# A reordered step in a one-core layer pipeline: three shared PSUM banks, a copied row buffer, a folded normalisation

## What is computed

```python
x = _ln(src) * (1.0 + scale) + shift          # scale, shift from the timestep
q, k, v = x @ Wq + bq, x @ Wk + bk, x @ Wv + bv
scores = q @ k.T / 4 + attention_bias         # per entry and head, 256 x 256
scores = where(src_mask, -inf, scores)
ctx = softmax(scores) @ v
x = x + (ctx @ Wo + bo)
h = _ln(x) * g2 + beta2
return x + _gelu2(h @ W1 + b1) @ W2 + b2      # _gelu2(z) = z * sigmoid(1.702 z), 1024 wide
```

## Time and profile before

| | us |
|---|---|
| median of 3 runs (lowest, highest) | 1541.29 (1540.1, 1541.68) |
| the profiled execution: its time | 1540.95 |
| its span, first to last instruction | 1539.2 |

### The profile page before, as it was taken

How to read it: one execution, slowest core, us unless ns; L and a number is a source line. 1 busy time by engine, 2 the same in 40 slices (tenths; PEclk the granted TensorE clock), 3 DMA queues, 4 the chain that set the end, 5 groups by cost and what they waited for, 6 DMA issues and landing times.

```text
span 1539.2 us, 37068 instructions
## 1 busy us (share of the span) xinstructions
PE 1305.6 (85%) x9217; PEld 1126.9 (73%) x9217; DVE 1207.3 (78%) x3280; ACT 979.0 (64%) x2358; POOL 722.3 (47%) x629
## 2 busy tenths in 40 slices
PE   2666599999999999982799998898988889999985
PEld 2555488888888888872678777777776777878875
DVE  3887899999999999976577777676775776777763
ACT  2222488888888888850666666565664666666761
POOL 1677488888888888863122223221332132222111
PEclk9999999999999999995899999898999999999997
DMA  3675333333343343326765566454663565556510
GB/s 113 226 238 198 134 130 127 126 132 124 125 133 125 124 133 126 129 81 221 227 188 184 160 196 189 149 168 141 186 201 124 172 185 165 173 166 188 172 56 14
DMA packets 195251, 236.53 MB, mean 154 GB/s; under 512 B 20448, under 2 KB 176288, under 8 KB 195168
## 3 DMA queue, kind: packets, MB, share of 16 engines
q1 hardware_dynamic: 182512, 198.51, 41.4%
q10 hardware_dynamic: 6480, 20.32, 4.1%
q0 software_dynamic: 6176, 16.79, 3.2%
HBM read 195.84 MB, written 39.71 MB: 153 GB/s over the span
## 4 chain that ended last, share of the span: by engine, by line
PE 29%; ACT 8%; DVE 8%; issue 7%; POOL 1%; SPq 1%; DVEq 0%; ACTq 0%; DMA 0%; POOLq 0%
PE ps_p L1258 5%; PE ps_g L1369 5%; PE ps_g L1326 4%; ACT bias L1158 4%; PE ps_ctx L1274 3%; PE ps_s L1244 3%; DVE bias L1459 2%; PE ps_g L1359 2%; PE ps_g L1315 2%; PE ps_s L1246 2%; DVE up_f L1542 2%; PE ps_g L1296 1%; ACT act_hi L1203 1%; PE ps_g L1316 1%; POOL act_lo L1117 1%
## 5 line engine op out<-in xcount | busy, mean ns | idle before, releaser
L351 POOL TENSOR_TENSOR w_lo<-w,w_hi 128x512 fp32r<-128x512 f32 x284 | 422.6, 1518 | 100.4 <-ACT w_hi L412 100.4
L1158 ACT ACTIVATE bias<-bias,neg_max 128x256 f32<-128x256 f32 x512 | 255.6, 501 | 203.9 <-DVE neg_max L1459 202.3
L714 DVE TENSOR_TENSOR w_lo<-w,w_hi 128x512 fp32r<-128x512 f32 x284 | 302.1, 1102 | 1.0 <-ACT w_hi L406 1.0
L1459 DVE CUSTOM_DVE_ANT_0 bias<-ps_s,bias 128x256 f32<-128x256 f32 x512 | 193.2, 415 | 32.2 <-issue 20.9
L412 ACT ACTIVATE w_hi<-w 128x512 fp32r x284 | 179.3, 633 | 54.0 <-PE ps_y L507 35.9
L1099 POOL TENSOR_TENSOR rstd<-mv,minus_half 128x2 f32<-128x2 f32 x32 | 23.1, 723 | 391.2 <-DVE mv L1517 305.4
L1244 PE MATMUL ps_s<-mask_f,minus_ident 128*128 128x256 f32 x512 | 156.6, 327 | 48.2 <-DVE neg_max L1459 31.0
L406 ACT ACTIVATE w_hi<-w 128x512 fp32r x284 | 173.3, 633 | 21.5 <-DVE tile_tab L683 11.0
L1258 PE MATMUL ps_p<-const,bias 128*128 128x128 f32 x1024 | 163.1, 283 | 23.8 <-ACT bias L1158 22.1
L507 PE MATMUL ps_y<-w_hi,hidT_hi 128*128 128x256 f32 x568 | 168.9, 297 | 14.9 <-DVE hidT_lo L700 14.2
L1117 POOL TENSOR_TENSOR act_lo<-up_f,act_hi 128x512 fp32r<-128x512 f32 x64 | 84.3, 1318 | 188.3 <-ACT act_hi L1203 188.3
(11 more groups left out here) (244 smaller groups left out, 3380.0 us busy)
## 6 DMA issues: line engine op xcount, KB each, us to landing
bias<-bias_dram SPq DMA_DIRECT2D x128, 512.0 KB, 3.7
b_row<-b_dram SPq DMA_DIRECT2D x71, 512.0 KB, 3.5
w<-w_dram ACTq DMA_DIRECT2D x32, 512.0 KB
xin<-dispatch SPq DMA_DIRECT2D x71, 128.0 KB, 2.2
b_row<-b_dram SPq DMA_DIRECT2D x71, 128.0 KB, 3.1
expert_out<-xin SPq DMA_DIRECT2D x71, 128.0 KB, 1.7
q_stack<-q_hi_rows SPq DMA_DIRECT2D x64, 128.0 KB, 3.3
k_stack<-k_hi_rows SPq DMA_DIRECT2D x64, 128.0 KB, 3.4
```

The source lines that it names most:

```text
L351: pool.tensor_tensor(w2_part["lo"][:, k, :], w2_piece(e, k), w2_part["hi"][:, k, :].bitcast(F32), ALU.subtract).then_inc(sem("w2_split"), 1)
L714: dve.tensor_tensor(w1_part["lo"][:, k, :], w1_piece(e, k), w1_part["hi"][:, k, :].bitcast(F32), ALU.subtract).then_inc(sem("w1_split"), 1)
L1158: act.activation(head_rows(h, j), head_rows(h, j), ACT.Exp, scale=-1.0, bias=neg_max[par][:, h, j:j + 1], accum_out=total[par][:, h, j:j + ...
L1459: dve.tensor_tensor_reduce(head_rows(h, j), ps_s[h % 2][:, j * T:(j + 1) * T], head_rows(h, j), -1.0, LARGEST, ALU.add, ALU.min, neg_max[p ...
```

## The change

- General banks: `ps_g` (2) and one of the two context banks give way to `ps_out`, `ps_k`, `ps_q`; the feed-forward's pairs use `ps_q` and `ps_k` (`ps_up`). The context of both halves goes to one bank.
- Order of a step on PE: q at 0, k at 2, `output` at 3, `values` at 4, `turn_h` at 6, `feed_up` at 7 to 10 as before, `feed_down` at 11 to 14, `turn_x` of entry n+2 at 15. On the other engines what follows moves with it: `modulate` of n+2 at 15; `upper` and `lower` of q at 1 and of k at 3; `scale_ctx` at 2; `combine_first` at 11, `combine_second` 12, `input_moments` 13, `normalise` 14; `finish` of entry n-1 at slot 15 of the same step rather than slot 0 of the next. `BY_VECTOR` has five heads.
- The modulated rows `xmT` have one buffer instead of two; a DMA on SP copies them to `xmT_kept`, from where `output` takes them.
- POOL's step: `take_mask`, `gather`, `rsqrt` of `rstd2`, `prepare_sum` (from DVE), the four `lower_gelu`, `rsqrt` of `rstd`. SP's step: `keep_rows` and `send_parts` come ahead of `load_bias(n, 6)`, and `bring_stacks` ahead of `load_bias(n, 7)`; what stands ahead of `load_mask` is as before.
- g2, beta2 and b1 are folded into W1 once: each row of W1 is scaled by g2, and the sum of b1 and beta2 - g2 times W1, over D, is added to each row, while `take_hT` adds 1 to the normalised rows, whose sum over D is nought. So `take_up` and `take_hT`'s scale and shift go, `tanh` and `gelu` read PSUM, and `take_hT` is one instruction that writes the upper part. The fold takes one more 512 KB load, four PE matmuls, and seven DVE instructions, in step -1, slot 6; `prepare_rest` moves there from slot 14.

```diff
...
-BY_VECTOR = (2, 3, 13, 15)
+BY_VECTOR = (0, 7, 8, 9, 10)
...
-    xmT = [sb(f"xmT{i}", [P, C, T]) for i in range(2)]
+    xmT = sb("xmT", [P, C, T])
+    xmT_kept = [sb(f"xmT_kept{i}", [P, C, T]) for i in range(2)]
...
-    ps_ctx = [bank(f"ps_ctx{i}") for i in range(2)]
-    ps_g = [bank(f"ps_g{i}") for i in range(2)]
+    ps_ctx = bank("ps_ctx")
+    ps_out, ps_k, ps_q = [bank(n) for n in ("ps_out", "ps_k", "ps_q")]
+    ps_up = [ps_q, ps_k]
+    b1_row = probT[:, 0:2, :, :].rearrange("p h j t -> p (h j t)")
+    less_gain = probT[:, 2, :, :].rearrange("p j t -> p (j t)")[:, 0:C * P].rearrange("p (c m) -> p c m", c=C)
...
+        def keep_rows(n, par):
+            sp.wait_ge(sem("xmT_ready"), C * (n + 1))
+            wait_free(sp, sem("wo_done"), n - 1, alone=True)
+            sp.dma_start(xmT_kept[par][:], xmT[:]).then_inc(sem("xm_kept"), 16)
...
                 if starting:
                     load_bias(n + 1, 0)
+                keep_rows(n + 1, 1 - par)
+                send_parts(n + 1)
             if exists(n):
                 load_bias(n, RING + 2)
             if exists(n + 1):
-                send_parts(n + 1)
+                bring_stacks(n + 1, 1 - par)
             if exists(n):
                 load_bias(n, RING + 3)
-            if exists(n + 1):
-                bring_stacks(n + 1, 1 - par)
             if exists(n + 1):
                 for c in range(1 if starting else 0, RING):
                     load_bias(n + 1, c)
...
+        def prepare_sum(n):
+            pool.wait_ge(sem("x3_ready"), n + 1)
+            wait_free(pool, sem("out_sent"), 16 * n)
+            pool.tensor_tensor(x3b[:], x3[:], spread(b2[:], [P, J, D], 1), ALU.add).then_inc(sem("x3b_ready"), 1)
         def step(n, par):
+            if exists(n + 1):
+                take_mask(n + 1, 1 - par)
+            if exists(n + 2):
+                gather(n + 2)
             if exists(n - 1):
                 rsqrt(rstd2, mv2, "var2_ready", "rstd2_ready", n - 1)
-            if exists(n + 2):
-                gather(n + 2)
-            if exists(n + 1):
-                take_mask(n + 1, 1 - par)
-            if exists(n - 1):
+                prepare_sum(n - 1)
                 for pair in range(4):
                     lower_gelu(n - 1, pair)
             if exists(n + 2):
...
-        def modulate(n, par):
+        def modulate(n):
             act.wait_ge(sem("xnT2_done"), n + 1)
             act.wait_ge(sem("entry_cols"), 4 * (n + 1))
-            wait_free(act, sem("wo_done"), n - 1)
+            wait_free(act, sem("v_done"), n)
+            wait_free(act, sem("xm_kept"), 16 * n)
             for c in range(C):
-                act.activation(xmT[par][:, c, :], ps_g[1][:, c * T:(c + 1) * T], ACT.Identity, bias=mod_now[:, 1, c:c + 1],
+                act.activation(xmT[:, c, :], ps_k[:, c * T:(c + 1) * T], ACT.Identity, bias=mod_now[:, 1, c:c + 1],
                                scale=mod_now[:, 0, c:c + 1]).then_inc(sem("xmT_ready"), 1)
...
         def take_hT(n):
             act.wait_ge(sem("h_turned"), n + 1)
-            wait_free(act, sem("hT_split"), n)
-            for c in range(C):
-                act.activation(hT[:, c, :], ps_g[1][:, c * T:(c + 1) * T], ACT.Identity, bias=vec[:, LN2_B + c:LN2_B + c + 1],
-                               scale=vec[:, LN2_G + c:LN2_G + c + 1]).then_inc(sem("hT2_ready"), 1)
+            wait_free(act, sem("ff1_done"), 4 * n)
+            act.activation(hT_part["hi"][:], halves(ps_k[:, :]), ACT.Identity, bias=1.0).then_inc(sem("hT_upper"), 1)
         def tanh(n, pair):
-            act.wait_ge(sem("up_ready"), F * n + 2 * pair + 2)
+            act.wait_ge(sem("ff1_done"), 4 * n + pair + 1)
             wait_free(act, sem("gelu_ready"), 4 * n + pair - 1)
             at = 2 * pair % 4
-            act.activation(tanh_f[:, at:at + 2, :], up_f[:, at:at + 2, :], ACT.Tanh, scale=0.851).then_inc(sem("tanh2_ready"), 1)
+            act.activation(tanh_f[:, at:at + 2, :], halves(ps_up[pair % 2][:, :]), ACT.Tanh, scale=0.851).then_inc(sem("tanh2_ready"), 1)
...
+                    modulate(n + 2)
                 if exists(n + 1):
+                    if isinstance(n, int) and n == -1 and h == 1:
+                        act.wait_ge(sem("setup_done"), 1)
+                    if h == 1:
+                        upper(n + 1, "q", ps_q, q_b)
                     if h == 3:
-                        modulate(n + 1, 1 - par)
-                    if h == 4:
-                        upper(n + 1, "q", 1, q_b)
-                    if h == 5:
-                        upper(n + 1, "k", 0, vec[:, K_B:K_B + C])
+                        upper(n + 1, "k", ps_k, vec[:, K_B:K_B + C])
                 if exists(n - 1):
...
         def turn_inv(n):
             pe.wait_ge(sem("inv_ready"), n + 1)
-            wait_free(pe, sem("up_ready"), F * n)
+            wait_free(pe, sem("result_ready"), n)
...
+            pe.wait_ge(sem("xm_kept"), 16 * (n + 1))
             for j in range(J):
...
         def feed_up(n, pair):
             if pair == 0:
                 pe.wait_ge(sem("hT_split"), n + 1)
-            elif pair == 1:
                 if exists(n + 2):
                     pe.wait_ge(sem("v_ready"), J * (n + 3))
-            else:
-                pe.wait_ge(sem("up_ready"), F * n + 2 * (pair - 1))
+            elif pair >= 2:
+                pe.wait_ge(sem("gelu_ready"), 4 * n + pair - 1)
             for i in range(2):
...
+        def fold_norm():
+            pe.wait_ge(sem("less_gain_ready"), 1)
+            for i in range(2):
+                for c in range(C):
+                    last = pe.matmul(ps_p[i][:, :], less_gain[:, c, :], w1_raw[c][:, i * 512:(i + 1) * 512],
+                                     start=(c == 0), stop=(c == C - 1))
+            last.then_inc(sem("norm_folded"), 1)
...
                         output(n - 1, 1 - par)
                 if exists(n + 1):
+                    if isinstance(n, int) and n == -1 and h == 0:
+                        pe.wait_ge(sem("setup_done"), 1)
+                    if isinstance(n, int) and n == -1 and h == 6:
+                        fold_norm()
+                    if h == 0:
+                        query_or_key(n + 1, "q", wq, ps_q)
                     if h == 2:
-                        turn_x(n + 1)
+                        query_or_key(n + 1, "k", wk, ps_k)
                     if h == 4:
-                        query_or_key(n + 1, 1 - par, "q", wq, 1)
-                    if h == 5:
-                        query_or_key(n + 1, 1 - par, "k", wk, 0)
-                if exists(n - 1) and h == 6:
-                    turn_h(n - 1)
-                if exists(n + 1) and h == 6:
-                    values(n + 1, 1 - par)
+                        values(n + 1)
                 if exists(n - 1):
+                    if h == 6:
+                        turn_h(n - 1)
                     if 7 <= h < 11:
                         feed_up(n - 1, h - 7)
-                    if h >= 12:
-                        feed_down(n - 1, h - 12)
+                    if 11 <= h < 15:
+                        feed_down(n - 1, h - 11)
+                if exists(n + 2) and h == 15:
+                    turn_x(n + 2)
                 if h % GROUP == 1:
                     before, head = neighbour(n, h, -GROUP - 1)
                     if exists(before):
                         weigh(before, head // GROUP, par if head < H - GROUP else 1 - par)
...
         def split_hT(n):
-            dve.wait_ge(sem("hT2_ready"), C * (n + 1))
-            wait_free(dve, sem("ff1_done"), 4 * n)
-            dve.tensor_copy(hT_part["hi"][:], hT).then_inc(sem("hT_upper"), 1)
             dve.wait_ge(sem("hT_upper"), n + 1)
-            dve.tensor_tensor(hT_part["lo"][:], hT, hT_part["hi"][:].bitcast(F32), ALU.subtract).then_inc(sem("hT_split"), 1)
...
-        def take_up(n, pair):
-            dve.wait_ge(sem("ff1_done"), 4 * n + pair + 1)
+            dve.scalar_tensor_tensor(hT_part["lo"][:], halves(ps_k[:, :]), 1.0, hT_part["hi"][:].bitcast(F32),
+                                     ALU.add, ALU.subtract).then_inc(sem("hT_split"), 1)
+        def gelu(n, pair):
+            dve.wait_ge(sem("tanh2_ready"), 4 * n + pair + 1)
             wait_free(dve, sem("act_split"), 4 * n + pair - 1)
-            for i in range(2):
-                f = 2 * pair + i
-                dve.tensor_scalar(up_f[:, f % 4, :], ps_g[1 - pair % 2][:, i * T:(i + 1) * T], vec[:, FF_B1 + f:FF_B1 + f + 1], None,
-                                  ALU.add).then_inc(sem("up_ready"), 1)
...
-            dve.wait_ge(sem("tanh2_ready"), 4 * n + pair + 1)
             at = 2 * pair % 4
-            dve.scalar_tensor_tensor(up_f[:, at:at + 2, :], tanh_f[:, at:at + 2, :], 1.0, up_f[:, at:at + 2, :],
+            dve.scalar_tensor_tensor(up_f[:, at:at + 2, :], tanh_f[:, at:at + 2, :], 1.0, halves(ps_up[pair % 2][:, :]),
...
```

(64 more changed lines are left out.)

78 lines of the change are left out of this document (36 added, 42 removed).

## The result

The changed kernel takes 1616.15 us (median of 4 runs, 1612.97 to 1622.43) where the kernel before takes 1541.49 beside it: 1.0485 times as long, 95% interval 1.0449 to 1.0522. Its profiled execution took 1622.43 us, 6 above its median, with a span of 1620.7 and a mean granted clock of 0.932 (before 0.967). The forecast was 1625.

The account below looks back on a forecast made before the run. PE sets the pace, but POOL's late root would hold it up: 13 x 54.0 + 4 x 4.5 = 720.0 instead of 639.8, +80.2, and +3.4 elsewhere, on 1540.95 give 1624.6, or 1625 us (1595 to 1660).

Parts of the forecast that it names:

- POOL's list decides: In POOL's step, `rstd2` stands behind late mask and gather, so `normalise2` ends at 24.1 while PE idles from 17.6.
- my upper end: Mask's landing after SP issues it: 3.0 us taken, upper value 3.7, as it starts behind bias chunk and result.
- Pure PE time and small waits, 40.5 + 1.05: Full step on PE: 40.5 us of work, plus waits of 0.25 for `xmT` and 0.8 for `feed_down`.
- rival 1: POOL is not late: `rstd2` answered at 14.6 to 15.5, step 43.2 us, total 1484, faster; chance 0.12.
- The delay, +9.4: Before `feed_up` in each full step: start at 28.4 instead of 18.95, +9.4 us, bounds 8.1 and 10.1.
- The clock, 3.0: PE's clock falls after 6.5 us idle ahead of `turn_h`, costing 3.0 us a step, bounds 0 and 5.
- rival 3: POOL late and PE at half clock through `feed_up`: 58 us a step, 1690 in all; chance 0.12.
- The step, 54.0: A full transformer step goes from 46.75 to 54.0 us, bounds 48.8 and 58.
- `feed_down`'s wait, 0.8 (0 to 1.4): PE's new wait at `feed_down`'s second quarter for the last `lower_gelu`: 0.8 us, less than 1.3 if `gelu` gets faster.
- The loop ends, 4 x 4.5 left: At four passes of the loop's end, 4.5 us each would remain of 7.8, between 1.3 and 7.8.
- The start, +11: Ahead of the first `minimum`, the fold's added work on DVE and PE delays the start by 11 us (9 to 14).
- Steps 14 and 15 and the tail, -7.6: Step 14, without `gather`, gains 1.6 us, step 15 gains 3, the last feed-forward 3.

Follow-up runs that it names:

- e12_after_again: The changed kernel, unchanged, run again beside the kernel before in a session on another chip: 1616.32 us, ratio 1.0342 to before.
- the fastest version: Changed kernel with POOL's root first, plus ACT taking `hT` and the last `upper_gelu` earlier and DVE the last lower part: 1480.51 us.

## Why the prediction was right, and where it was not

- **POOL's list decides: right, and shown from both sides.** Undoing it gains 119 us, doing it alone in the kernel before costs 54, or about 80 beside a before without ACT's unnamed wait. Counted from T0 = 1110.47, the chain ran: mask issued at 11.8 (forecast 11.1), taken by POOL 3.7 later (3.0, with 3.7 as the upper bound), `mask_f` 1.5, copies and gather 6.5, root 0.75, `turn_h` at 26.0 (24.1). The rest of that difference is one term I had at 0.73: the two normalisations, the second of which is held up beside POOL's `prepare_sum`, took 1.67. That this is the cause, the sum moved late shows: 0.73 again.
- **"DMA: Bandwidth & Descriptors", Two DMAs through the same engine are not ordered.** The Trainium skill's rule put the landing nearer to my upper end, and the trace agrees: counted as in the earlier trace rows, the mask landed in 3.5 us in the median (shortest 3.4), where a bias chunk took 3.6 in the same trace and 3.7 in before.
- **Pure PE time and small waits, 40.5 + 1.05: too low by 4.1.** Without the delay a step takes 45.66, of which PE is busy 42.32 and idle 3.3. The busy time counts the tail of a matmul ahead of each wait, which I had put to the waits, so how the 4.1 divide between the two terms isn't settled; taken as they stand, they are 1.8 and 2.3. Slot by slot I was a little short: slots 1 to 6 begin at 3.2, 6.5, 9.0, 12.9, 15.5 and 17.9 us, forecast 3.0 to 16.7, and with the root first PE starts `turn_h` at 19.5 and not at 17.6. DVE's variance, forecast for 14.6, was there at 17.05. For the same reason rival 1 (1484) was 13 us too fast: its mechanism was tried and gave 1497.36.
- **The delay, +9.4: in truth 7.6** of `feed_up`'s start against the kernel with the root first (29.16 against 21.59 behind `turn_inv`). The first figure was against a start without any wait, 18.95, which PE can't reach.
- **The clock, 3.0: half of that, 1.4**, as measured with the clock held up. I had taken off a part of the slow time for the chain; more of it lies under the chain than I thought. The drop came as forecast, behind an idle time of 6.4 us, and rival 3 (low through all of `feed_up`) didn't come: it was back at 1.00 by 1144.
- **The step, 54.0: 54.6.** 42.3 + 3.3 of waits + 7.6 + 1.4. My terms for PE and its small waits were 4.1 too low, those for the delay and the clock 3.5 too high. That they cancel to 0.6 is luck: the mechanism was right, and the sum is better than its parts.
- **`feed_down`'s wait, 0.8 (0 to 1.4): 1.23**, and `xmT` 0.20 (0.25). The first is within its bounds, though `gelu` did get as fast as I hoped (0.68 us instead of 1.29 in the median).
- **The loop ends, 4 x 4.5 left: 0 left.** The term was mis-sized, by 18 us in the sum, for a reason I didn't see, that DVE's instructions aren't loaded again in the changed kernel. The argument itself (if DVE alone stops, PE's wait shrinks to 1.3 and the clock stays) held as far as it was tried: with the loads forced back, the stall costs 0.8 to 1.2 us a time and the clock stays, but that stall was 2.3 us and not 4.0. The Trainium skill ("Runtime: NRT & Kernel Launch", Instruction fetch mechanics) says that a taken branch stalls when its target isn't in the fetched pages; that fits the queue's loads in rounds with a stall and their absence in rounds without one, but the length at which it begins is not the listed count: 284 instructions reload in one kernel and don't in another.
- **The start, +11: +10.2, and part of it for another reason.** DVE's first `minimum` came at 739.89, not at 744 to 747, so only 5.4 us of the delay stood there, and 4.8 came up to the first full step. With the root first and the fold kept, that step begins at 777.55, 779.33 and 779.50 in three traces, 5.0 to 6.9 later than before; with the root late at 782.80 here and at 779.74 in `e12_after_again`. So most of it is there without POOL's order, and the scatter between traces is too wide to say what that order adds.
- **Steps 14 and 15 and the tail, -7.6: -2.0.** Step 14 gained nothing, step 15 1.7 instead of 3, and the last feed-forward 0.3 instead of 3 in this trace. In `e12_after_again` it gained 2.6, and step 14 lost 1.5, which sums to nearly the same. No run looked into this.
- **Sum.** Forecast +83.6 on the profiled execution, measured +81.5; on the medians +74.7, since the profiled execution was the slowest of its four. So the forecast is 9 us high, and the 18 us for the loop ends, which didn't come, are more than that.

## What to carry to other kernels

Before moving an instruction in a list, write down when its inputs come and, for everything moved in front of it, when that one's come too: here a 64 KB load that another queue issues fifth in its step held up a root of 256 numbers, and with it the whole core. When a long step becomes 1 us shorter and nothing happens, look at the granted clock ahead of looking for a new wait; and read a stall's price from whether it reaches the engine that sets the pace, not from its length alone. Fillers and additions to a loop's body are not free even where the engine is idle: compare the instruction queues' loads.

## What the runs showed of the hardware

- **Loop bodies and instruction loads.** PE's queue had 28 loads in all; with 20 and with 48 instructions more in the loop's body it had 66, and PE stood 0.8 to 3.2 us of "issue" at a time. DVE's queue had 34 with bodies of 282 and 284 instructions (as listed for the expectations), 55 with 301 and 302, and 75 with another body of 284. Moving the body by 40 instructions changed nothing. The rule behind this is open.
- **A DVE instruction can wait for POOL inside its own duration.** Beside POOL's addition of two SBUF tiles, the second of the two normalisations took 1.35 us instead of 0.37 (durations in ns: shortest, median, longest of the two):

```profile
L1547 DVE TENSOR_SCALAR h_rows<-x,mv,rstd x2: 401/874/1347, 1134.7 to 1136.0; 128x256 f32<-128x256 f32 x2
```

  The Trainium skill ("SBUF — State Buffer", SBUF: two separate sides) describes a port pair that one of the two engines holds for a whole instruction; the trace agrees for the second normalisation, as DVE's 1.35 end 0.5 us behind POOL's instruction, and taking that away brought the 0.73 back. The first one ran its 0.40 beside the same POOL instruction without harm, by the rows' starts, which on POOL are rough.
- **Less idle time, longer at half clock.** 6.38 us of idle time were followed by 7.4 us at 0.51, 5.42 us by 9.3 us at 0.50. In the idle time itself the clock was 0.77 and 0.60 in the mean, which makes 2.9 and 4.3 us of half clock there.
- **One kernel, several chips.** The kernel before differed by 1.4 to 1.9% between comparisons on different chips, with one wait of ACT of up to 2.7 us, that names no engine, in most steps of the slower traces; the changed kernel didn't differ. The wait isn't in every kernel on such a chip: not in before with the root last, and in the fastest version it stands at another instruction. Whether it goes by chip or by time no run tells.
